# Window mixing on one core: VectorE's additions of a half image in a row, the norm's scale between the first and the second

## The reference

```python
def _gn(v, G=32, eps=1e-05):                 # groups of 8 channels
    m = mean over (group's channels, H, W); s = var over the same
    return (v - m) / sqrt(s + eps)
x = x + _L0_conv_ref(_gn(x), L0_conv_w, L0_conv_b)   # windows of 8x8, shifted by 4, 16 heads:
                                                     # y[i] = sum_j w[head, i, j] * window[j] + b[head, i]
x = x + _L1_conv_ref(_gn(x), ...)                    # qkv projection, 5x5 and grouped 1x1 convolutions,
                                                     # linear attention, projection, batch norm
```

## Time and profile before

| | |
|---|---|
| median of 3 runs | 2447.16 us (2444.57 to 2449.64) |
| the profiled execution | 2445.44 us, span in the profile 2443.7 us |
| TensorE's mean granted clock | 0.991 |
| window mixing, by the timeline | from 0 to about 255 us |
| busy share of the whole span: PE, DVE, ACT, POOL | 96%, 82%, 61%, 45% |

### The profile page before, as it was taken

How to read it: one execution, slowest core, us unless ns; L and a number is a source line. 1 busy time by engine, 2 the same in 40 slices (tenths; PEclk the granted TensorE clock), 3 DMA queues, 4 the chain that set the end, 5 groups by cost and what they waited for, 6 DMA issues and landing times. The chain is left out here.

```text
span 2443.7 us, 65297 instructions
## 1 busy us (share of the span) xinstructions
PE 2343.0 (96%) x25485; PEld 1867.1 (76%) x25485; DVE 1996.5 (82%) x2655; ACT 1492.5 (61%) x1863; POOL 1087.9 (45%) x1475
## 2 busy tenths in 40 slices
PE   5989899999999999899999999999999899999998
PEld 5888787888888887677888888888888656666666
DVE  7888778878888876888888888888888688888885
ACT  5888666666666665666676667677676434433333
POOL 6722477778778877000000000000000068888887
PEclk9999999999999999999999999999999999999999
DMA  7874699988998999987888888888888767777774
GB/s 283 348 304 177 219 308 335 352 306 312 337 320 301 350 312 299 247 198 197 207 214 207 206 210 208 211 208 206 209 209 212 239 236 280 276 276 275 275 276 138
DMA packets 300952, 628.19 MB, mean 257 GB/s; under 512 B 50784, under 2 KB 252256, under 8 KB 291552
## 3 DMA queue, kind: packets, MB, share of 16 engines
q1 hardware_dynamic: 295072, 590.38, 78.4%
q10 hardware_dynamic: 4688, 31.63, 3.6%
q0 software_dynamic: 1008, 3.67, 0.4%
HBM read 327.81 MB, written 300.94 MB: 257 GB/s over the span
## 5 line engine op out<-in xcount | busy, mean ns | idle before, releaser
L1583 PE MATMUL c_ps<-dh,wh 128*128 128x512 f32 x1152 | 463.0, 402 | 11.8 <-DVE wl L1738 9.6
L1498 ACT ACTIVATE dh<-image 128x1632 fp32r<-128x1632 f32 x192 | 301.7, 1572 | 265.0 <-PE c_ps L1583 251.3
L1583 PE MATMUL c_ps<-dh,wl 128*128 128x512 f32 x1152 | 455.0, 395 | 0.0
L1583 PE MATMUL c_ps<-dl,wh 128*128 128x512 f32 x1152 | 453.4, 394 | 0.0
L1946 POOL TENSOR_TENSOR ql<-image,qh 128x1024 fp32r<-128x1024 f32 x1 | 2.4, 2358 | 961.7 <-DVE ql L2180 961.7
L1691 DVE TENSOR_TENSOR dl<-image,dh 128x1632 fp32r<-128x1632 f32 x192 | 356.4, 1856 | 72.4 <-ACT dh L1498 72.4
L1145 PE MATMUL o_ps<-xh,wqh 128*128 128x512 f32 x768 | 317.5, 413 | 1.0 <-DVE xl L1237 0.6
L1934 POOL TENSOR_TENSOR ql<-image,qh 128x1024 fp32r<-128x1024 f32 x126 | 301.5, 2424 | 9.0 <-ACT qh L1967 9.0
L1145 PE MATMUL o_ps<-xl,wqh 128*128 128x512 f32 x768 | 301.5, 393 | 0.0
L1145 PE MATMUL o_ps<-xh,wql 128*128 128x512 f32 x768 | 300.3, 391 | 0.9 <-issue 0.9
L1583 PEld LDWEIGHTS c_ps<-dh,wh 128*128 128x128 f32 x1152 | 217.3, 189 | 63.8 <-DVE wl L1738 9.7
(11 more groups left out here) (212 smaller groups left out, 5081.8 us busy)
## 6 DMA issues: line engine op xcount, KB each, us to landing
qkv_scratch<-stage SPq DMA_DIRECT2D x384, 408.0 KB, 5.0
image<-qkv_scratch SPq DMA_DIRECT2D x189, 816.0 KB, 6.3
yq_scratch<-qy SPq DMA_DIRECT2D x64, 512.0 KB, 6.7
image<-qr_scratch SPq DMA_DIRECT2D x128, 256.0 KB, 6.1
image<-yq_scratch SPq DMA_DIRECT2D x128, 256.0 KB, 5.3
ox<-x_scratch SPq DMA_DIRECT2D x8, 4096.0 KB, 15.0
qr_scratch<-qs SPq DMA_DIRECT2D x126, 256.0 KB, 4.0
out<-ox SPq DMA_DIRECT2D x7, 4096.0 KB, 12.7
```

What stands on the lines that cost most here:

```text
L1498: act.activation(by_image(dh[kind]), as_loaded(kind), ACT.Copy).then_inc(hi_ready, 1)
L1583: last = pe.matmul(c_ps[:, m, :], w[hp][:, kind, part, o:o + P], d[kind][:, n0:n0 + IMG * HALF * NB], start=(k == 0), stop=(k == 5))
```

## The change

In DVE's loop over the steps of `window_mixing`: the call of `scale()` that stood before the first addition stands behind it. Where it stood, one more statistics piece is issued (only at the steps with a chain). The piece that followed each of the four additions is gone from there; what is left of the eight pieces follows behind the last addition, in the loop that was already there.

```diff
@@ -730,10 +730,11 @@
                     variance()
                 next(pieces, None)
                 if image is not None:
-                    scale()
+                    next(pieces, None)
                 for n in range(BACKS):
                     add_back(s, n)
-                    next(pieces, None)
+                    if n == 0 and image is not None:
+                        scale()
                 for _ in pieces:
                     pass
```

## The result

The changed kernel takes 2459.24 us (median of 10 runs, 2450.23 to 2464.03) against 2448.74 us before (10 runs, 2443.45 to 2453.38): ratio 1.0037, 95% interval 1.0026 to 1.0048. It is slower by 0.37%, where the forecast was 4.1 us and "within 0.2%"; the range ended at 2457. The profiled execution takes 2457.34 us, 11.9 more than before.

The account below looks back on a forecast made before the run. The prediction took PE to be held by DVE's additions at g = 0 and DVE's unbroken work from g = 1 to g = 0. Its terms, -4.9 + 7.7 + 1.3 = +4.1 us, gave 2451.2 us, range 2446 to 2457.

Parts of the forecast that it names:

- What bounds mixing, and where: Window mixing: DVE's late additions hold PE at g = 0; DVE, never idle, sets the way from g = 1 to g = 0.
- g = 0, -4.9 us: Steps with g = 0: addition 1 ends 0.78 us earlier in six steps, 0.2 us at (6,0); together -4.9 us.
- g = 1, +7.7 us: Steps with g = 1: additions wait for turn_backs, more pieces stand behind them, aggregation 1.1 us later, seven times; +7.7 us.
- PE then waits longer for the bias: At g = 1: PE's 0.36 us wait for addition 3 goes but gives nothing back, as the bias wait grows.
- SP's queue: SP's stores and loads in mixing: the store is issued earlier and so is the load behind it; cost nothing.
- nameless stalls: Two mixes where PE stands still, 2.1 us in all: taken as 0, bounds -2.1 to +7.4 us.
- The last step, +1.3 us: Step (7,1): later aggregation delays the link, and the scale now stands behind addition 0; additions end at 255.3 us, +1.3 us.
- the reading as instruction fetch: PE's unexplained standstills in mix: read as instruction fetch behind a store, one 1.3 us after the store was issued.
- The rivals: Mixing: DVE slack, faster (chance 0.08); bias holds PE, slower (0.24); stores hit fetch oftener, slower (0.14); step kinds cancel (0.06).
- The bias at g = 1: Rival, slower: four pieces behind g = 0 additions delay the bias, 0.2 us lost in six steps; 2452.5 us; chance 0.24.

Follow-up runs that it names:

- delay2: Kernel before with two more statistics instructions on DVE (1.2 us) at the end of each g = 1 step, ahead of the aggregation; ratio 1.0049.
- after_half: Changed kernel with images 3 to 7 loaded by one half of their channels only; projections' first matmul at 263.43 us.
- after_half_fill8: Changed kernel with half loads of images 3 to 7 and 8 filling matmuls in PE's wait for the bias; projections' first matmul at 255.42 us.
- g0_only: Kernel before with the new order only at the seven g = 0 steps that have a chain; ratio 0.9998.
- before_half: Kernel before with images 3 to 7 loaded by one half of their channels only; projections' first matmul at 252.58 us.
- after_fill16: Changed kernel with 16 filling matmuls on PE behind mix, where it otherwise waits for the bias; ratio 1.0037.

## Why the prediction was wrong

- **What bounds mixing, and where.** Right: PE's waits for additions at g = 0, and DVE's unbroken tail from g = 1 to the next g = 0. delay2 shows the second by itself.
- **g = 0, -4.9 us.** Right in its mechanism and a little low: 12.9 us instead of 13.8 per distance, 0.9 where 0.78 was forecast; -5.7 us with the loads out of the way.
- **g = 1, +7.7 us.** The waits of additions for turn_backs and the seven later aggregations are there, 7.2 us with the clock held up. The step that failed is "PE then waits longer for the bias", to which the prediction gave the wait's own length as its price. A wait of PE has a second price where the granted clock falls behind it: +8.0 us, as the pair after_half and after_half_fill8 shows. The rows of before held a warning: the clock was 1.00 in all of mixing, so every duration in the sum was one at full clock, and no term asked what a PE with 2.4 us of waits in a row (1.76, 0.42, 0.25) would be granted. The Trainium skill, TensorE: Matmul & The Clock Gate, "HAM oscillation — how this bites in real kernels", describes a kernel that drops its clock at a gap that returns with every tile; these runs agree with it in kind. In size they don't: the page puts the fall down to single gaps longer than any wait in these kernels' mixing with half loads, and here the clock fell behind places whose longest wait is 1.76 to 1.97 us.
- **SP's queue: "the store is issued earlier", "and so is the load behind it. Cost nothing."** Wrong: in g0_only a store comes 2.5 us earlier and the load behind it 1.3 us later, as the store and the load before it are then in flight together. In g0_only the transfers cost more than the term gains (M 259.27 against 247.11 with half loads). In the changed kernel little of it shows: DVE's waits for loads behind the first image are 0.6 us. That the longer tail at g = 1 gives the loads time is my reading, not a run's. With half loads the loss is 10.9 us, with full loads 12.2, so 1.3 us is left to loads and nameless stalls.
- **The last step, +1.3 us.** Right: the tail from turn_back 0 to M grows by 1.06 us (1.48 in the half-load pair, with a short fall of the clock in it).
- **The nameless stalls, taken as 0.** Right in size in the changed kernel (1.9 us in mix after, 2.1 before). They are gone in before_half (M 2.8 us earlier), which ties them to DMA traffic. The traces also support the reading as instruction fetch. The stall of before that ends at 137.53 has a 16 KB transfer of the queue marked "instruction" ahead of it, from 135.10 to 136.04, right behind the store issued at 134.90. In all kernels with full loads each stall of over 0.3 us in mix ends 0.9 to 1.5 us behind such a transfer. In kernels with PE's program unchanged the stalls stand at three places only, with 38, 55 or 72 matmuls of a mix left; in those with filling matmuls, which move what follows them in the program, they stand elsewhere (47 left in after_fill16). No run changed the fetch alone.
- **The rivals.** None was it. The bias at g = 1 held PE for 0.24 to 0.43 us in three steps of the changed kernel (two times DVE's part, once ACT's), each behind a low clock; in distances of 12.9 us it did not.

## What to carry to other kernels

When an edit makes a PE that is nearly always busy wait longer, price the wait twice: its length, and the clock of the matmuls behind it; where the trace before shows only full clock, that second price has no row and needs a bound (here 8.0 us beside 7.2 us of later aggregations). Before pieces are taken out from between paced instructions, see what sets the pace: if the piece has the length of the wait that would stand in its place, it is free there and not free behind. And where the next load waits for a store, a store that comes earlier need not bring the load earlier; count the transfers that are in flight when it starts.

## What the runs showed of the hardware that I had not expected

- The granted clock falls to its lower level behind waits of PE that are short against mixing's step of 14 us. The changed kernel has waits of 1.76, 0.42 and 0.25 us close together. With half loads the clock falls behind six of seven such places, which costs 8.0 us of M; 8 filling matmuls in the first of the three waits keep it up at all of them, and one fall is left, at 246.9 us in the last step.
- A 128x128 matmul of f32 by f32 takes 0.23 us where a turn of the same size (transpose) takes 0.11.
- A store of 2 MB issued 3.4 us behind a load of 2 MB in the same queue took 11.6 us until the next load could start, where one issued 6.6 us behind took 7.7: issued 2.5 us earlier, it was done 1.3 us later.
